# Clearing the semaphores of ended stages at three places instead of at 44 in a two-layer perceiver kernel

## The reference, cut to what matters

```
x = x + L0_xattn(layernorm(x), ctx)     # 8 heads over 1601 context rows of 384
x = x + L0_attn(layernorm(x))           # rotary self attention
x = x + L0_ffn(layernorm(x))            # 8 experts, 2 per token, width 512, gated
x = x + L1_xattn(layernorm(x), ctx)     # top-32 attention, film, a long convolution by FFT
                                        # matrices, a feed-forward of width 2048, layernorms
x = x + L1_attn(layernorm(x))           # 16 heads, causal
x = x + L1_ffn(layernorm(x))            # 8 experts, 2 per token, width 2048, and a layernorm
```

## The kernel before, in words

| place, start in the trace (us) | lists | names |
| --- | --- | --- |
| first norm, 15.3 | 2 | 1, 4 |
| `cross_attention_L0`, queries, 46.0 | 1 | 5 |
| the same, main stage, 553.2 | 1 | 18 |
| the same, output, 581.0 | 3 | 6, 6, 7 |
| `self_attention_L0`, 636.3 | 3 | 13, 14, 4 |
| `moe_L0`, 832.5 | 7 | 3, 7, 20, 20, 4, 9, 2 |
| norm `n3`, 842.7 | 2 | 1, 4 |
| `top_attention`, 1137.8 | 4 | 24, 4, 13, 4 |
| `film`, 1189.5 | 1 | 11 |
| `mixing`, 1221.9 | 2 | 5, 2 |
| `feed_forward`, 1330.5 | 4 | 17, 4, 4, 3 |
| norm `n8`, 1339.6 | 2 | 1, 4 |
| `self_attention_L1`, 1486.3 | 2 | 22, 2 |
| `moe_L1` and the program's own, 1865.3 | 10 | 3, 7, 20, 20, 4, 4, 9, 1, 2, 1 |

## Time and profile before

### The profile page before, as it was taken

How to read it: one execution, slowest core, us unless ns; L and a number is a source line. 1 busy time by engine, 2 the same in 40 slices (tenths; PEclk the granted TensorE clock), 3 DMA queues, 4 the chain that set the end, 5 groups by cost and what they waited for, 6 DMA issues and landing times. The chain is left out here.

```text
span 1870.0 us, 23575 instructions
## 1 busy us (share of the span) xinstructions
PE 1695.7 (91%) x8822; PEld 1307.9 (70%) x8822; DVE 980.1 (52%) x1498; ACT 582.0 (31%) x1056; POOL 340.1 (18%) x294
## 2 busy tenths in 40 slices
PE   7899999999998989867999988989699998999994
PEld 4899999999975777743565656568586564666761
DVE  1668677686765534345999996463525320000004
ACT  4454434534522111003444522044236321111110
POOL 0530433123300010021555541100100010000002
PEclk9899999999998999978998988989899998999996
DMA  4331223132205456537254350520200193696832
GB/s 127 106 106 53 70 89 107 53 96 63 93 29 198 180 180 237 183 99 257 71 204 153 125 204 1 197 91 0 92 1 1 35 368 140 231 330 212 318 107 77
DMA packets 111217, 246.95 MB, mean 132 GB/s; under 512 B 14024, under 2 KB 43736, under 8 KB 106472
## 3 DMA queue, kind: packets, MB, share of 16 engines
q1 hardware_dynamic: 101952, 225.17, 34.7%
q10 hardware_dynamic: 6568, 11.54, 1.8%
q0 software_dynamic: 2560, 8.39, 1.4%
HBM read 225.68 MB, written 19.40 MB: 131 GB/s over the span
## 5 line engine op out<-in xcount | busy, mean ns | idle before, releaser
L371 PE MATMUL x_s_ps<-x_cxt,x_qs 128*128 128x400 f32 (+1 forms) x1152 | 245.1, 358 | 10.0 <-POOL x_qs L344 5.9
L1090 PEld LDWEIGHTS e_ps<-e_xg,e_w 128*128 128x128 f32 x1792 | 208.8, 194 | 43.9 <-issue 42.1
L397 PE MATMUL x_o_ps<-x_cx,x_pt 128*128 128x386 f32 (+1 forms) x1248 | 230.3, 343 | 0.0
L1090 PE MATMUL e_ps<-e_xg,e_w 128*128 128x128 f32 x1792 | 212.4, 278 | 16.3 <-issue 14.6
L397 PEld LDWEIGHTS x_o_ps<-x_cx,x_pt 128*128 128x128 f32 (+1 forms) x1248 | 220.6, 190 | 1.4
L371 PEld LDWEIGHTS x_s_ps<-x_cxt,x_qs 128*128 128x128 f32 x1152 | 206.2, 192 | 11.2 <-issue 11.1
L1082 PE MATMUL e_ps<-e_w,xt 128*128 128x512 f32 x352 | 163.4, 606 | 0.9 <-ACT xt L1427 0.6
L2122 PE MATMUL x_s_ps<-x_cxt,x_qs 128*128 128x512 f32 (+1 forms) x384 | 144.2, 533 | 7.8 <-POOL x_qs L2318 5.8
L1310 DVE COPY e_y<-e_ps 128x512 f32<-128x512 f32 x20 | 13.7, 686 | 239.7 <-PE e_ps L1082 239.7
L2122 PEld LDWEIGHTS x_s_ps<-x_cxt,x_qs 128*128 128x128 f32 x384 | 68.9, 196 | 86.0 <-issue 80.1
L447 DVE TENSOR_TENSOR x_pt<-x_t_ps,x_pt 128x512 fp32r<-128x512 f32 (+1 forms) x128 | 74.6, 586 | 91.9 <-ACT x_pt L537 91.6
(11 more groups left out here) (385 smaller groups left out, 2731.4 us busy)
## 6 DMA issues: line engine op xcount, KB each, us to landing
e_w<-in_L_ffn_W SPq DMA_DIRECT2D x16, 4096.0 KB, 17.1
x_cxt<-in_ctxT SPq DMA_DIRECT2D x8, 2401.5 KB, 8.7
x_cx<-in_ctx SPq DMA_DIRECT2D x8, 2304.0 KB
e_w<-in_L_ffn_gate_up_proj SPq DMA_DIRECT2D x8, 2048.0 KB, 8.0
x_stage<-in_ctxT SPq DMA_DIRECT2D x16, 768.0 KB, 4.4
x_stage<-in_ctx SPq DMA_DIRECT2D x16, 768.0 KB, 6.0
e_w<-in_L_ffn_down_proj SPq DMA_DIRECT2D x8, 1024.0 KB, 9.3
ff_w<-in_L_xattn_W SPq DMA_DIRECT2D x2, 4096.0 KB
```

What stands on the lines that cost most here:

```text
L371: last = nc.tensor.matmul(s_ps[:, n, 0:b - a], qs[:, u % 2, p, c, :], cxt[:, q, c, a:b], start=(m + c == 0), stop=(m + c == len(PARTS) + C ...
L397: last = nc.tensor.matmul(o_ps[:, 0:WIDE], pt[0:rows, p, t, :], cx[0:rows, q, t, :], start=(t + m == 0), stop=(t + m == KT - 1 + len(PARTS ...
L1090: last = nc.tensor.matmul(u_ps[:, g % 2, a * PER + n, :], w1[:, e % PAIR, m, a * hidden + c * P:a * hidden + (c + 1) * P], xg[:, m, :], st ...
```

## The change

`sems` only notes the list for later. The stage's stack appends the names to `core.left_over` when it closes, and nothing is issued. A new method `clear` clears all names noted so far, frees them, and has one meeting. `build_program` calls it after `moe_L0`, after the L1 attention (when `hold` is closed), and at the end. A stage's semaphores therefore keep their numbers until then, and later stages take other numbers.

```diff
+        self.left_over = []
...
         made = [self.nc.alloc_semaphore(name=f"{stage}_{n}") for n in names.split()]
-
-        def release():
-            self.nc.clear_and_free_semaphores(made)
-            self.nc.all_engine_barrier()
-
-        ctx.callback(release)
+        ctx.callback(self.left_over.extend, made)
         return made
+
+    def clear(self):
+
+
+        self.nc.clear_and_free_semaphores(self.left_over)
+        self.nc.all_engine_barrier()
+        self.left_over = []
...
         moe_L0(core, x, xn, xt, w, sent, back)
+        core.clear()
         with ExitStack() as hold:
             weights = cross_attention_L1(core, norm("n3"), hold, x, xn, xt, k, ident, w)
             self_attention_L1(core, norm("n8"), x, xt, ident, w, weights)
+        core.clear()
         moe_L1(core, x, xn, xt, w, sent, back, out)
+    core.clear()
```

## The result

The changed kernel took 1870.20 us (median of 22 runs, 1860.03 to 1881.10), the kernel before 1873.37 us beside it (22 runs, 1864.99 to 1893.67). The ratio is 0.9951 with an interval of 0.9928 to 0.9974: 9.2 us less, somewhere from 4.9 to 13.5. So I go by the ratios with their intervals, and not by two medians. The direction was forecast, but 1870.2 lies above the range of 1843 to 1859 us, and 18.5 us above its middle value of 1851.7. The kernel before itself read 6.1 us higher in these runs than in the three that were shown; the other 12.4 us are a difference of medians of 3.2 in place of 15.6, of which 6.4 stay if the gain is read from the ratio.

A forecast was written before the change was run, and what follows sets the result against it. TensorE's matrix work bounds the kernel, busy 1695.7 of 1870.0 us. Releases 20.0, less 3.0 put back, 0.8 hidden, 0.6 hitches: 15.6 us less, median 1867.3 to 1851.7 us; 8-in-10 range 1843 to 1859 us.

The forecast's parts named there:

- The price of the 44 releases: All releases of the kernel before, taken as on the path, cost 20.0 us together, bounded by 19.1 and 20.5.
- Norm `n3`: Two releases there lie under a mask load issued ahead of them, so 0.8 us of gain is lost.
- TensorE's wait behind the output stage of `cross_attention_L0`: Sign: TensorE's wait before L674 should go from 2.3 to about 1.1 us.
- One range for each call: Each of the three new calls clears its names in one range; the three releases put back 3.0 us together.
- the first rival: Clears stay 44 and only meetings go, 0.2 us per list's flush and clear: 10.4 us less, 1856.9 us; chance 0.12.
- The hitches: About 1.1 us of the releases' 20.0 are queues' own pauses; half, 0.6 us, was expected to come back elsewhere.
- the stages that follow run longer by what was saved: Sign of a wrong prediction: stages behind the removed releases lengthen by the time saved; no size given.
- more than 3: Sign: the clear's line should show 3 clears instead of 44; more than 3 speak for the first rival.
- The gain eaten at half of the places: Rival: loads hide the gain at half the places, losing 6 to 8 us: 1859 us; chance 0.08, shared with one low stretch.
- the rival by the clock: Rival: clock rises after `cross_attention_L0`'s output stage and the last attention, up to 8.0 us more won: 1846 us; chance 0.13.
- The rival by one more low stretch: Rival: one more low-clock stretch at a stage's start costs 8.0 us, 1860 us; chance 0.08, shared with gain eaten by loads.

The follow-up runs named there:

- five-fold kernel: Kernel before with five meetings in each of its 44 releases instead of one, 176 more: 1938.06 us, ratio 1.0318.
- the one at the L1 attention: Kernel before with 30 more meetings at the place after the L1 attention alone: 1892.72 us, ratio 1.0068.
- the two with thirty meetings behind it: Kernel before with 30 more meetings, either at norm `n3` (1889.68 us, 1.0037) or after the L1 attention (1892.72 us, 1.0068).
- the two controls: Sorted changed kernel plus 40 DRAINs: on TensorE behind `moe_L0` (1870.44 us, 0.9942), or ahead of it on each of the four other queues (1870.99 us, 0.9949).
- the four with DRAINs ahead: Changed kernel padded everywhere (0.9911); sorted changed kernel with TensorE DRAINs just ahead of `moe_L0`: 10 (0.9913), 40 (0.9891), 40 again (0.9924).
- padded everywhere: Changed kernel with two TensorE DRAINs in place of each of the 41 removed releases, without meetings or clears: 1862.47 us, ratio 0.9911.

## Why the prediction was right in direction and wrong in size

**What was right.** The price of the 44 releases was 20.0 us, and the trace's full account is 20.50. That they lie on the path with their full length is shown by the five-fold kernel (59.9 us for 61.7) and by the one at the L1 attention (12.8 for 11.0). The gain is the meetings': with them back it was gone. Norm `n3` gives nothing (0.9 us lost, 0.8 forecast). TensorE's wait behind the output stage of `cross_attention_L0` fell from 2.3 to 1.0 us, 1.1 forecast. Stages with no low clock in either trace are equal to 0.01 us (the query and output stages of `cross_attention_L0`, 29.87 and 27.28 us in both), and its main stage, with some low clock in each, has 506.76 and 506.75 us. So new semaphore numbers cost nothing.

**One range for each call: wrong, and small.** Lists are noted as stacks close, and the numbers that the first call gave back are handed out in another order, so the later calls clear three and five ranges. What is put back is 4.4 us instead of 3.0. Sorted, it is 3.5; the rest is the longer flush. Each further flush and clear costs 0.15 us, (4.42 - 3.53) / 6, less than the first rival's 0.2.

**The hitches: wrong.** I gave 0.6 us back for queues' own pauses. The main account needs none: 20.5 - 4.4 is the whole change at the places.

**The step that failed: that the stages run on as they were.** The prediction costed what each removed instruction took and held the rest equal, with no term for it; it named as one sign of being wrong that "the stages that follow run longer by what was saved". One stage does run longer. Ten of the removed meetings stand ahead of `moe_L0`, two instructions each on TensorE's queue, and by these 20 its code moves up. The seventh expert's jump had its instruction packet in the kernel before, too, 1.6 us ahead of the end of the queue's last weight load; now the packet starts 1.9 us after the queue ran dry. From the releases ahead to its Block's end, `moe_L0` takes 196.5 us in the mean of five traces with the code in its old place (194.5 to 198.2: before twice, the two with thirty meetings behind it, the one with the meetings back), 199.7 in the mean of seven with the code moved (197.4 to 202.4: changed three times, sorted twice, the two controls), and 196.1 in the four with DRAINs ahead (192.4 to 198.6). That is 3.6 us between the families with the code moved and with DRAINs ahead, and 3.2 to the code's old place, though single traces overlap. The lateness of the seventh and eighth expert together sums to 5.3 us in the mean of the five and 8.1 in the mean of the seven, 2.8 us more. In the profiled pair it is 7.94 against 4.85 us, 3.1 more, and the stage is 199.6 against 194.5 us, 5.1 more; 3.0 us more of low clock lie in it.

The account is then 16.1 less, 0.9 hidden at `n3`, 3.2 lost in `moe_L0`: 12.0 us. The span of the profiled pair went down by 11.1 us. That this is so near is partly luck: its `moe_L0` lost 5.1 us and not 3.2, and other stages differ by as much either way (`top_attention` 2.5 us longer, the 0.9 of `n3` among them, `moe_L1` 2.1 shorter). By the times, the seven timed kernels with the code moved have a mean ratio of 0.9946, 10.2 us. The four with instructions ahead have 0.9910, 17.0 us, near the 15.6 that was forecast; their releases less the 0.9 at `n3` give 15.2 to 16.1. Beside each other on one chip they are 1862.5, 1866.4 and 1865.7 against 1869.8 us, and 1866.1 against the controls' 1870.4 and 1871.0: 3.5 to 7.3 us. The 6.8 us between the two families are more than 3.2; each kernel's interval is some 6 us to either side, so whether the low clock behind the late jump takes the rest isn't settled. Two of the four, with 10 DRAINs and padded everywhere, have the eighth expert's late jump still, like the kernel before.

**The range.** It was built from the spread of three runs, 2.8 us to either side. Single runs of the kernel before spread by 30 us, and its median was 6 to 17 us above the three's in the sets here. Even the kernels that save all that was forecast have medians of 1862 to 1866 us, above the range. An account of differences can be right to a microsecond and the absolute time be missed by ten.

**The rivals.** The clears that stay 44 came true in a small part: nine clears, by the prediction's own sign ("more than 3"), and worth 0.9 us. The gain eaten at half of the places is refuted: 0.9 us are hidden, at one place. The clock did rise, in the first pair of traces, where the rival by the clock looked: over the 30 us behind the last attention it is granted 0.89, before 0.72, and the mean is 0.946 against 0.941. But the changed kernel's third trace has a mean of 0.939, and the kernel before, traced again, is granted 0.83 over the 20 us behind the output stage of `cross_attention_L0`, where its first trace has 0.66. This wanders from trace to trace in both kernels, and nothing shows that the change does it. The rival by one more low stretch named about the right size, but not the cause: it held that gaps get shorter, and one grew by 3.5 us.

**The better version.** The three-place clear, sorted, with 40 idle instructions of TensorE ahead of `moe_L0`: 0.9891 and 0.9924 against the kernel before, where the change alone has 0.9943 to 0.9959. The intervals of the two overlap, and no run has it beside the sorted kernel without DRAINs; the two late jumps gone from the trace are the firmer evidence.

## What to carry to other kernels

Meetings of all engines cost their full length here wherever they stood on the path, 0.33 to 0.37 us each alone and 0.47 with a flush and a clear (59.9 us of time for 61.7 in the trace with 176 more of them, 12.8 for 11.0 with 30 more): look them up by their line, since no busy row shows them, and expect less where a transfer issued ahead is awaited behind, as at `n3`, where 5.5 of 10.7 us lay under the mask's landing. In a program with jumps by a register, an edit that takes instructions off a queue also moves its code, and here 20 fewer ahead of `moe_L0` went with a lateness of 4.27 us in place of 0.82 at the seventh expert's jump: look for waits ended by "issue" at the jumps, for long COMPARE_BRANCH records and for the instruction packets ahead of them, and test with a few idle instructions before you judge the edit. Clear semaphores in order of their numbers: here that made three clears of nine, and 3.53 us of releases in place of 4.42.

## What the runs showed of the hardware that was not expected

TensorE's queue stood still for 3.5 to 4.8 us at a jump (21 cases): the 16 KB packet starts 1.0 to 2.4 us after the queue ran dry, and the next instruction, the count's load, comes 2.4 to 2.6 us after its start. Ten or twenty instructions more or less ahead decided it: at the seventh expert the lateness is 0.6 to 1.1 us in the five traces with the code in its old place, 3.5 to 4.6 in the seven with 20 instructions fewer ahead, and 0.50 with 10 DRAINs added to those. Why the packet starts late isn't shown. In the changed kernel's seventh expert TensorE's granted clock fell from 1.00 to 0.50 between 768.40 and 768.80 us, towards the end of this standstill, and the 32 matmuls behind took 6.66 us in place of 3.83.

A range clear took 44 ns for one name (L53, at norm `n3` before), and 413 for 71, 716 for 125 and 810 for 143 (L58, names sorted). The flush ahead of it grew with it: 66 ns there, then 168, 232 and 282.
